# Conditioned sequence block on one Trainium2 core: order of the adapter weight pieces in the prologue

## The reference, cut to what matters

```python
# layer 0: attention with 16 heads of 16, then SwiGLU, both after an RMS norm scaled and shifted by cond
x = x + a_alpha * attention(ada_rmsnorm(x, t, ...), W_q, W_k, W_v, W_o)
x = x + f_alpha * swiglu(ada_rmsnorm(x, t, ...), gate_w, hidden_w, out_w, out_b)
# layer 1: gated MLP, its activations rounded to 8 bits by their row maxima, its down weights to -1, 0, 1
# layer 2: adapter, weights made per batch out of h_lang = cond (the "hyper" product)
dWd = ((h_lang @ Wdd.T + bdd) * 0.1).reshape(B, 128, 256)
dWu = ((h_lang @ Wdu.T + bdu) * 0.1).reshape(B, 256, 128)
down = relu(einsum('bld,bnd->bln', x, Wd + dWd) + bd)
x = x + einsum('bln,bdn->bld', down, Wu + dWu) + bu
# layer 3: layer norm plus tanh(cond @ lin_w.T + lin_b)
```

## Time and profile before

| | us |
|---|---|
| three timed runs | 1100.28, 1100.31, 1108.78 |
| their median | 1100.31 |
| the profiled execution's own time | 1104.08 |
| its span, first to last instruction | 1102.3 |
| prologue up to the landing of the first stack | 0 to 38.6 |
| stage 0 up to the first exponential | 38.6 to 63.4 |
| stage 0 up to the first gate product of stage 1 | 63.4 to 100.5 |
| stage 1 up to its first `scores` | 100.5 to 133.3 |
| stage 1 up to the end of its last up product | 133.3 to 174.3 |

### The profile page before, as it was taken

The page is one execution under the profiler, slowest core; times in us unless marked ns, Lnnn a source line. Parts: engine busy times, 40 slices in busy tenths (PEclk is TensorE's granted clock), DMA queues, the critical chain, the costliest instruction groups (busy, mean ns, idle before and its releaser), DMA issues.

```text
span 1102.3 us, 22357 instructions
## 1 busy us (share of the span) xinstructions
PE 998.7 (91%) x7426; PEld 848.2 (77%) x7426; DVE 751.0 (68%) x1711; ACT 547.8 (50%) x1144; POOL 194.5 (18%) x250
## 2 busy tenths in 40 slices
PE   5585889999999999999999999999999999998965
PEld 4243669797888979797978889797979788896953
DVE  4735458676777768786767777777867677766552
ACT  3163454655555554646555555546465555545430
POOL 1411511021120202010211202020101112020210
PEclk9587989999999999999999999999999999999985
DMA  8983532040404021120404040211304040300000
GB/s 293 296 307 125 202 148 75 13 124 2 135 1 127 8 91 44 49 85 9 125 1 134 1 125 9 87 48 45 89 2 133 1 134 1 120 7 15 6 20 10
DMA packets 78049, 89.45 MB, mean 81 GB/s; under 512 B 18672, under 2 KB 64640, under 8 KB 75392
## 3 DMA queue, kind: packets, MB, share of 16 engines
q1 hardware_dynamic: 72368, 63.86, 19.3%
q0 software_dynamic: 2304, 16.78, 4.1%
q10 hardware_dynamic: 3344, 8.39, 2.3%
HBM read 63.14 MB, written 25.31 MB: 80 GB/s over the span
## 4 chain that ended last, share of the span: by engine, by line
PE 68%; DVE 10%; issue 9%; ACT 5%; DMA 3%; POOL 2%; SPq 1%; ACTq 0%; DVEq 0%; POOLq 0%
PE bank L645 15%; PE bank L600 14%; PE bank L614 7%; PE bank L561 5%; PE bank L545 5%; PE bank L571 4%; PE bank L505 3%; PE bank L579 3%; PE bank L663 3%; ACT probs L874 2%; PE bank L683 2%; PE bank L677 2%; PE bank L624 1%; DVE den_x L1160 1%; DVE den_x L1162 1%
## 5 line engine op out<-in xcount | busy, mean ns | idle before, releaser
L874 ACT ACTIVATE probs<-bank 128x512 f32<-128x512 f32 x256 | 138.3, 601 | 66.5 <-PE bank L561 65.7
L462 POOL TENSOR_TENSOR act_lo<-act_f,act_hi 128x256 fp32r<-128x256 f32 x128 | 95.7, 753 | 421.8 <-ACT act_hi L916 421.8
L1129 DVE TENSOR_REDUCE neg_max<-bank 128x2 f32<-128x512 f32 x256 | 161.9, 681 | 0.0
L910 ACT ACTIVATE silu_g<-bank 128x256 f32<-128x256 f32 x128 | 49.1, 384 | 190.0 <-PE bank L600 189.9
L561 PE MATMUL bank<-q_stack,k_stack 128*128 128x256 f32 x512 | 98.5, 315 | 12.3 <-ACT probs L874 11.8
L645 PE MATMUL bank<-up_hi,h_hi 128*128 128x256 f32 x512 | 108.8, 294 | 0.6 <-DVE act_u L1234 0.3
L953 ACT ACTIVATE gelu_g<-bank,r 128x256 f32<-128x256 f32 x128 | 60.7, 474 | 95.6 <-PE bank L645 94.8
L600 PE MATMUL bank<-h_hi,gh_hi 128*128 128x256 f32 x512 | 103.5, 284 | 4.6 <-DVE h_lo L1190 4.6
L645 PE MATMUL bank<-up_lo,h_hi 128*128 128x256 f32 x512 | 103.3, 283 | 0.0
L600 PE MATMUL bank<-h_lo,gh_hi 128*128 128x256 f32 x512 | 103.2, 283 | 0.0
L600 PE MATMUL bank<-h_hi,gh_lo 128*128 128x256 f32 x512 | 103.0, 283 | 0.0
(11 more groups left out here) (158 smaller groups left out, 2127.2 us busy)
## 6 DMA issues: line engine op xcount, KB each, us to landing
hyper<-w_hyper POOLq DMA_DIRECT2D x16, 1024.0 KB, 6.2
q_stack<-q_dram SPq DMA_DIRECT2D x96, 128.0 KB
k_stack<-k_dram SPq DMA_DIRECT2D x96, 128.0 KB
q_dram<-probs SPq DMA_DIRECT2D x16, 512.0 KB, 2.8
k_dram<-probs SPq DMA_DIRECT2D x16, 512.0 KB, 3.6
x_res<-xT SPq DMA_DIRECT2D x16, 256.0 KB, 2.8
out<-xc SPq DMA_DIRECT2D x16, 256.0 KB, 2.5
x_in<-xT SPq DMA_DIRECT2D x15, 256.0 KB, 2.7
```

The costliest lines, as they stand in the source:

```text
L462: pool.tensor_tensor(act_lo[:, c % 3, :], act_f[:, c % 2, :], act_hi[:, c % 3, :].bitcast(F32), ALU.subtract).then_inc(g_lo.sem, 1)
L874: act.activation(probs[:, h % SLOTS], halves(SCORE_BANKS[h % 3]), ACT.Exp, scale=float(H / D) ** 0.5).then_inc(s_exp.sem, 1)
L910: act.activation(silu_g[:, c % 2, :], halves(4 + c % 2)[:, 0, :], ACT.Silu).then_inc(g_silu.sem, 1)
L1129: dve.tensor_reduce(neg_max[:, qt, :, pair:pair + 1].rearrange("p a o -> p (a o)"), halves(n % 3), AX_X, ALU.max, negate=True).then_inc(ma ...
```

## The change

- POOL no longer loads pieces 0 and 1 in the prologue. It makes the low parts 0 and 1, waits for the first stack, loads pieces 0 to 5, makes low part 2, and loads 6 to 9.
- PE no longer multiplies pieces 0 and 1 in the prologue. Products 0 and 1 stand at c = 4 and c = 6 of stage 0 (behind `max_scores` 15), 2 and 3 at c = 9, 4 and 5 behind `attend` 1 and 2, 6 and 7 behind `project_qk(nxt)` and ahead of `project(a)`. `norm_a(nxt)` of stage 0 moves from c = 8 to behind `attend` 0.
- ACT evicts all 16 pieces and stores them. In stage 0 it evicts piece 0, makes high part 2, evicts piece 1, and only then copies the row of maxima; 2 and 3 follow, 4 and 5 stand behind exponentials 9 and 13, 6 and 7 behind `split_qk(nxt)`. The square and the guess of `norm_a(nxt)` move behind exponentials 3 and 7.
- Stage 1 has products 8 to 15 at c = 0, 1, 3, 4, 5, 6, 7, 8, none behind the `attend`s. POOL waits after `act_lo(0)` for the second stack, and then loads one piece after each of `act_lo` 0, 1, 3, 4, 5, 6: pieces 10 to 15. In ACT's order the square of `norm_a(nxt)` and the two bias additions to `x1` (L904) move from c = 1 and 2 to c = 6.
- DVE and SP lose the four evictions and the four stores.

```diff
@@ -259,11 +259,10 @@
...
         hyper_in = [sem(f"hyper_in{i}") for i in range(4)]
-        hyper_mm, hyper_ev, hyper_ev_dve = sem("hyper_mm"), sem("hyper_ev"), sem("hyper_ev_dve")
+        hyper_mm, hyper_ev = sem("hyper_mm"), sem("hyper_ev")
         hyper_out = [sem(f"hyper_out{i}") for i in range(4)]
         TABLE = 9 + 3 * DC
-        RUN1 = (0, 1, 4, 5, 8, 9)
-        HYPER_DVE = range(4, 8)
+        RUN0, RUN1, LOADS1 = (4, 6), (0, 1, 3, 4, 5, 6, 7, 8), (0, 1, 3, 4, 5, 6)
         TERNARY = 4 + 3 * 4
...
@@ -391,10 +390,6 @@
...
                                          max_rows[NPAIR * par:NPAIR * (par + 1), :].bitcast(F32)).then_inc(max_dma.sem, 16)
-                    if starts(a):
-                        for n in HYPER_DVE:
-                            sp.wait_ge(hyper_ev_dve.sem, n - HYPER_DVE[0] + 1)
-                            hyper_store(sp, n)
                     if nxt:
...
@@ -461,13 +456,12 @@
...
                                                ALU.subtract).then_inc(g_lo.sem, 1)
-                            if starts(f) and c in (1, 3):
-                                hyper_load(9 + c)
-                                hyper_load(10 + c)
+                            if starts(f) and c == 0:
+                                pool.wait_ge(stack_dma.sem, stack_dma.at(a))
+                            if starts(f) and c in LOADS1:
+                                hyper_load(10 + LOADS1.index(c))
                     if starts(f):
                         low_part(3)
-                        hyper_load(14)
-                        hyper_load(15)
                         low_part(4)
...
@@ -487,15 +481,14 @@
...
                 pool.memset(k_stack[:].bitcast(F32), 0.0).then_inc(init_pool.sem, 1)
-                pool.wait_ge(raw_in[1].sem, 16)
-                for n in range(2):
-                    hyper_load(n)
                 low_part(0)
...
                 pool.wait_ge(stack_dma.sem, stack_dma.at(Batch(0)))
-                for n in range(2, 10):
+                for n in range(6):
                     hyper_load(n)
                 low_part(2)
+                for n in range(6, 10):
+                    hyper_load(n)
                 whole(pool, run)
...
@@ -691,17 +684,11 @@
...
 
-                def by_act(n):
-                    return n if n < HYPER_DVE[0] else n - len(HYPER_DVE)
-
                 def hyper_product(n):
...
                     if n >= 2:
-                        if n - 2 in HYPER_DVE:
-                            pe.wait_ge(hyper_ev_dve.sem, n - 2 - HYPER_DVE[0] + 1)
-                        else:
-                            pe.wait_ge(hyper_ev.sem, by_act(n - 2) + 1)
+                        pe.wait_ge(hyper_ev.sem, n - 1)
                     for j in range(4):
...
@@ -731,7 +718,7 @@
...
                             max_turn(a)
-                        if nxt and c == FC:
+                        if nxt and c == FC and not starts(a):
                             if f:
...
@@ -739,8 +726,11 @@
...
                             max_scores(a, 15)
-                        if starts(a) and c in (7, 9):
-                            hyper_product(c // 2 - 1)
+                        if starts(a) and c in RUN0:
+                            hyper_product(RUN0.index(c))
+                        if starts(a) and c == FC + 1:
+                            hyper_product(2)
+                            hyper_product(3)
                         if starts(f) and c in RUN1:
...
@@ -765,10 +755,10 @@
...
                             attend(a, t)
-                        if starts(a):
-                            hyper_product(4 + t)
-                        if starts(f) and t >= 2:
-                            hyper_product(12 + t)
+                        if starts(a) and t == 0:
+                            norm_a(nxt)
+                        if starts(a) and t in (1, 2):
+                            hyper_product(3 + t)
                         if g and t < 3:
...
@@ -779,6 +769,9 @@
...
                         ln_mean(g)
+                    if starts(a):
+                        hyper_product(6)
+                        hyper_product(7)
                     if a:
...
@@ -813,9 +806,6 @@
...
                 cond_products(range(2, 8), bank[5])
-                for n in range(2):
-                    hyper_product(n)
-
                 pe.wait_ge(table.sem, TABLE - 1)
...
@@ -971,7 +961,7 @@
...
                     act.activation(hyper_s[n % 4], bank[6 + n % 2][:], ACT.Copy, scale=0.1).then_inc(hyper_ev.sem, 1)
-                    act.wait_ge(hyper_ev.sem, (n if n < HYPER_DVE[0] else n - len(HYPER_DVE)) + 1)
+                    act.wait_ge(hyper_ev.sem, n + 1)
                     hyper_store(act, n)
...
@@ -992,15 +982,17 @@
...
                         raw_load(2)
-                        hyper_out_piece(2)
+                        hyper_out_piece(0)
+                        high_part(2)
+                        hyper_out_piece(1)
                     if f:
...
                             silu(f, c)
-                        if nxt and c == 1:
+                        if nxt and not starts(a) and c == (6 if starts(f) else 1):
                             square_a(nxt)
-                        if f and c == 2:
+                        if f and c == (6 if starts(f) else 2):
                             bias_x1(f)
...
@@ -1009,14 +1001,13 @@
...
                     act.preload_act_table_set("natural_log_exp_and_others")
-                    if nxt:
+                    if nxt and not starts(a):
                         guess_a(nxt)
                     if starts(a):
+                        hyper_out_piece(2)
                         hyper_out_piece(3)
...
                         raw_load(4)
-                    if starts(f):
-                        hyper_out_piece(13)
                     for t in range(4):
...
@@ -1025,16 +1016,17 @@
...
                                 guess_g(f)
+                            if starts(a) and h == 3:
+                                square_a(nxt)
+                            if starts(a) and h == 7:
+                                guess_a(nxt)
+                            if starts(a) and h in (9, 13):
+                                hyper_out_piece(4 + (h - 9) // 4)
                             if f and h == 9:
                                 hi_g(f)
-                    if starts(f):
-                        hyper_out_piece(14)
                     if a:
                         den_guess(a, 0)
-                    if starts(f):
-                        hyper_out_piece(15)
                     if starts(a):
-                        high_part(2)
                         high_part(3)
...
@@ -1043,6 +1035,8 @@
...
                     if starts(a):
+                        hyper_out_piece(6)
+                        hyper_out_piece(7)
                         high_part(4)
...
@@ -1085,8 +1079,6 @@
...
                 high_part(1)
-                for n in range(2):
-                    hyper_out_piece(n)
                 whole(act, run)
...
@@ -1313,11 +1305,6 @@
...
                     newton(b, y4, 6, EPS_LN, n4_dve, 2)
-
-                def hyper_evict(n):
-                    dve.wait_ge(hyper_mm.sem, n + 1)
-                    dve.wait_ge(hyper_out[n % 4].sem, 16 * (n // 4))
-                    dve.tensor_scalar(hyper_s[n % 4], bank[6 + n % 2][:], 0.1, None, ALU.mult).then_inc(hyper_ev_dve.sem, 1)
 
...
@@ -1348,14 +1335,8 @@
...
                         relu(g)
-                    if starts(a):
-                        for n in HYPER_DVE[:2]:
-                            hyper_evict(n)
                     if a:
                         normalise(a, 0)
-                    if starts(a):
-                        for n in HYPER_DVE[2:]:
-                            hyper_evict(n)
                     if f:
...
```

## The result

| | before | after |
|---|---|---|
| median of 10 runs each, same chip, us | 1105.82 (1100.28 to 1108.78) | 1110.99 (1106.55 to 1114.69) |
| ratio | | 1.0059, 95% interval 1.0033 to 1.0085 |
| the profiled execution's own time (span) | 1104.08 (1102.3) | 1106.55 (1104.7) |

The changed kernel is slower by 0.6%. That is within the 1% called no change, but its time lies above the predicted range, and the difference has the other sign: +5.2 us by the medians where -1.0 was forecast. Seven more runs of the kernel before also moved its median from 1100.31 to 1105.82, so of the 11.7 us between 1110.99 and the forecast of 1099.3, 5.5 come from the base: two of the three runs shown were the lowest of the ten. The other 6.2 us are the forecast's error on the change itself. Read as differences, the predicted range was -5.8 to +5.2 us, and the measured +5.2 stands at its upper end.

What follows compares the result with a forecast made beforehand. PE was taken as the bound from stage 2 on and in stage 1's chunk loop, other waits in stage 0. Terms -8.0 + 9.9 - 2.9 = -1.0 us on 1100.31 gave 1099.3, range 1094.5 to 1105.5.

Steps and rivals of the forecast that it cites:

- the row of maxima 4.15: Stage 0: from the end of ACT's copy of the row to the first scores takes 4.15 us, scores at 58.1.
- the stack's wait 0.4: Stage 1's first maxima: a new wait for the second stack of 0 to 1.5 us, taken as 0.4.
- the 1.3 gained by DVE's rounding: Prologue: DVE's twelve rounding instructions end at 41.4 instead of 42.65, 1.3 us gained, bounds 0 and 3.1.
- the 1.0 for the half clock: Stage 1 chunk loop: idle gaps bring work at half clock, 1.0 us added (0 to 3.2).
- the waits for pieces: Stage 1 chunk loop: PE waits 0.5, 2.1 and 3.6 us for pieces 10, 12 and 14, 6.2 us in all.
- The turn: Stage 0, `max_turn` behind DVE's 16 maxima: due at 52.8 us, where it was 52.3, so nothing gained.
- piece 0 was there in time: Stage 0: piece 0 is wanted at 46.7 us and taken as landed; otherwise 2.7 us late on the path.
- L: Stage 1 chunk loop: landing time of a piece's load, taken as 5.7 us; each 0.1 costs 0.3.
- The part about ACT's biases: Stage 1, piece 14: square and two biases (0.6 + 0.9 us) ahead of `act_high(5)` make the wait 3.6.
- The row of maxima in stage 1: Stage 1: the row, copied behind eviction 14, makes PE wait 1.3 us.
- Behind the loop: Stage 1 heads: ACT's eviction 13 leaves the front of the exponentials, 0.8 us gained of a wait of 2.09.
- A: Stage 1 waits for pieces 10, 12, 14: L is 6.8, adding 3.3 us plus 1.6 half clock; 1104.2, chance 0.27.

Runs made afterwards that it cites:

- b2: b1 with POOL's low parts 0 and 1 moved behind DVE's rounding and the first four loads; ratio to the kernel before 0.9931, median 1097.38 us.
- e1: Changed kernel's new prologue and stage 0 with the stage 1 of before; ratio to the kernel before 0.9978, median 1103.51 us.
- e5: Changed kernel with the loads of pieces 4 and 5 moved behind low part 2; ratio to the kernel before 1.0017, median 1108.34 us.
- b3: b2 with ScalarE's 1 MB raw load behind eviction of piece 0, high part 2 behind that of piece 3; ratio to kernel before 0.9965, 1101.18 us.
- e2: Changed kernel with POOL issuing each stage 1 load ahead of its wait for ACT's high half; ratio to the kernel before 1.0014, median 1107.32 us.
- e6: Changed kernel without POOL's wait for the second stack ahead of load 10; ratio to the kernel before 1.005, median 1111.8 us.
- b1: New stage 0 with old stage 1, stores 6 and 7 behind stage 1's first SiLU, loads 4 and 5 behind low part 2; ratio to kernel before 0.9945, 1099.01 us.
- e3: Changed kernel with ACT's square and two biases back at chunks 1 and 2 of stage 1; ratio to the kernel before 1.008, median 1114.68 us.

## Why the prediction was wrong

Up to stage 2 the forecast was -1.0 and the profile has +5.7: 6.7 us missed, 2.7 ahead of gate 0, 3.2 in the loop, 0.8 behind it. The steps that failed are the two small transfers on the path, taken to last as long or to be as well covered as before (the row of maxima 4.15 and the stack's wait 0.4, measured 6.0 and 2.62), the 1.3 gained by DVE's rounding (measured 0) and the 1.0 for the half clock (2.8). The large term, the waits for pieces, was right (6.2, measured 6.7).

**DVE's rounding: "1.3 gained".** It gained nothing. The prediction let the first instruction begin at 31.2 and POOL's low parts end at 37.9, where they were. They began at 32.17, and POOL ended 1.5 later (39.4): it started 0.9 later and its eight instructions took 10.78 us instead of 10.21 (9.84 in b2, with none of DVE's rounding beside them). The lower bound, 0, was the right one. In the b2 kernel, where nothing of POOL overlaps, the twelve take 5.7 us, so what held them was POOL and not the wait for PE. The turn slipped by 1.1 with it (53.9, predicted 52.8). That piece 0 was there in time was luck: the prediction wanted it at 46.7, and it was used at 48.39, 9.05 us after its issue; in e1, where PE did wait for it (0.46 us), it took 9.6. To be there at 46.7 it would have had to land within 7.4 us, so with the rounding's gain product 0 would probably have waited.

**The row of maxima: "needs 4.15".** It needed 6.0, and this is the largest part of the miss ahead of gate 0: 1.1 from the rounding and 1.9 from here put the scores at 61.03 and not at 58.1. In the kernel before one load had gone out 2.3 us ahead of it (55.22 and 57.55); in the changed one there are two, 4.5 and 1.2 us ahead. The prediction moved the step and kept its duration. e5 shows it by taking them away (2.76), b3 by putting another in their place (6.05). From the scores on, the steps held: 18.1 us to the end of `attend` 3 (18.3 predicted), `project` without a gap, 10.5 us from there to gate 0 (10.2).

**The second stack: "0 to 1.5, I take 0.4".** It was 2.62. By the prediction's own numbers, 14.7 us from the start of `project` and 2.7 from gate 0 to the first maxima, with the marks that came out: the stack due at 84.67 + 14.7 = 99.4, wanted at 95.2 + 2.7 = 97.9, a wait of 1.5, the upper bound (1.3 by the true time of wanting, 100.74 - 2.62 = 98.1). The kernels with late stores have 1.28 to 1.56; I took 0.4 though no row stood closer to it. It is there because `project` and the gates come closer together than the DMAs behind `project` can follow. The rest, 1.1 to 1.3, is the two stores, 1.07 us between the write and the read back, which now stand in just that stretch and which the prediction didn't set against the stack.

**The waits for pieces: "6.2".** They were 0.74, 2.01 and 3.99, 6.7 in all (0.5, 2.1 and 3.6 predicted). The mechanism was right, POOL's order and two slots, and e2 confirms it by taking them away. That only the even pieces wait held in the changed kernel and not in e6. L was 6.1, 5.5 and 6.1 us, 5.9 on the mean for 5.7. By the Trainium skill, DMA: Bandwidth & Descriptors, section Anatomy of one DMA, it would be an estimated 4.4 for the megabyte; no load in these chains was as short, the least was 4.92 (b1). The part about ACT's biases was right as a wait (3.99 to 1.87 in e3) and wrong as a gain.

**The row of maxima in stage 1: "1.3 of waiting".** There was none. Its DMA was hidden behind what PE had left once piece 14 had been waited for. This error went the other way.

**Half clock: "1.0 (0 to 3.2)".** What is left of the loop is 45.9 - 32.8 - 2.1 + 1.1 - 2.6 - 6.7 = 2.8 us. The mean granted clock fell from 0.91 to 0.86, that is from 5.9 to 12.9 us at the lower level (the share missing to 1.0, doubled, times the length), 7.0 us more, in which up to 3.5 us of work at full clock are lost. So 2.8 fits, near the upper bound. PE's busy time says the same: 36.51 - 31.65 = 4.9 us more, 2.1 of them the two products, the other 2.8 the same matmuls taking longer. No run holds the clock fixed.

**Behind the loop: "0.8 of a wait of 2.09".** The wait of the first exponentials of stage 1 stayed, 2.22 us. So the 0.8 us were not gained; that ACT's eviction 13 had made the old wait is refuted.

Of the rivals, A (the loop loses more, 1104.2) comes nearest, with its place right and its cause wrong: it put 3.3 us on L, which added 0.5 us. The two small transfers, the row of maxima and the stack, are the largest part of the miss, 4.1 of 6.7 us; without them the trace would still stand at about +1.6, so they alone don't make the sign. Both share the DMA engines with transfers that the change issues around them. The prediction looked at the large loads as something waited for, and not as something that others wait behind.

## What to carry to other kernels

When a step is moved forward, list what its DMAs and stores will be in flight beside: a small transfer on the path (two DMAs of 8 KB here) took 5.8 to 10.1 us beside two megabyte loads, and 2.76 without. Removing a wait of an engine gained nothing here while a neighbour stretched its instructions threefold; look at the duration of the instructions after the wait, not only at the wait. With two slots and one load per chunk, issue the load as soon as the slot is free, and reckon the bytes per chunk against what the DMA engines move: here 347 GB/s were asked for, and the loop still waited for transfers when they were issued as soon as their slots were free. And compare kernels by marks that all share, up to where the change ends: code that nobody touched moved gate 0 by 1.9 us and the last stage by 7.5 us between executions.
